# Six PSUM banks shared out anew in a cross-attention loop: four for scores, two for maxima, and one exponential instruction per key chunk

## The chip, the cores and the metric

The kernel runs on one core of a Trainium2 chip. The time is the duration of the whole program on the device in microseconds. Before the change its median is 2073.19 us of 3 runs (2069.59 to 2075.86).

## What is computed

Four transformer-like layers work on x (16 batches x 56 tokens x 128 features), a condition vector per batch, and a context of 16 batches x 1500 keys x 128. Layer 0 has a one-head attention over the context and a small mixture of experts. Layers 1, 2 and 3 each hold a cross-attention of 16 heads of 8 features over the 1500 keys; layers 2 and 3 have a self-attention and a feed-forward part as well. The cross-attentions are what the change touches. In layer 3:

```python
def mha(q_in, k_in, v_in, qw, qb, kw, kb, vw, vb, ow, ob):
    Q = (q_in @ qw + qb).reshape(Bq, Lq, H, DH)          # 16 x 56 x 16 x 8
    K = (k_in @ kw + kb).reshape(Bq, Lk, H, DH)          # 16 x 1500 x 16 x 8
    V = (v_in @ vw + vb).reshape(Bq, Lk, H, DH)
    scores = jnp.einsum('bqhd,bkhd->bhqk', Q, K) / np.sqrt(DH).astype(np.float32)
    attn = jax.nn.softmax(scores, axis=-1)
    out = jnp.einsum('bhqk,bkhd->bqhd', attn, V).reshape(Bq, Lq, D)
    return out @ ow + ob

x = _L1_xcond_ref(x, ctx_1024, cond_1024, ...)   # cross-attention
x = _L2_xcond_ref(x, cond_1024, ctx_1024, ...)   # self, cross, feed-forward
x = _L3_xcond_ref(x, ctx_1024, cond_1024, ...)   # self, cross, feed-forward
```

## The kernel before

Every engine has its own instruction list, written out in one fixed order, and semaphores join the lists. There is no scheduler: an engine that waits at an instruction holds back everything behind it.

A cross stage (`cross`, once per layer 1, 2, 3) treats 16 batches one after another. While batch b is attended, the maxima of batch b+1 ("following") are found, and the keys and values of batch b+2 ("behind") are prepared. The loop `attend` has C = 12 slots, one per chunk c of 125 keys. Its parts:

- **Scores** (`scores`, L1119). Per chunk, 4 matmuls of 224 columns, one for each group of 4 heads, write 125 keys x 896 (head, token) columns. The 896 columns are two halves of HR = 448, and each half fills most of one PSUM bank. The halves go round a ring of SC_RING = 3 banks (banks 0 to 2): half u of chunk c is in bank (2c + u) % 3. A half waits (L1117) until the exponential that read its bank last is done.
- **Exponentials** (`ACT.Exp`, L768). ScalarE takes each half out of PSUM into `probs` (an SBUF ring of 4 chunks, named `q_parts` in the trace) with one instruction: two per chunk. No maximum is subtracted here; it is already within the scores, through two more rows of the stacked queries `q_st`.
- **Values** (`values`, L1093). 8 small matmuls per chunk (16 instructions) add the chunk's part of the output into bank 6. At every even slot from 2 on, the values of the two chunks before it are done together.
- **Maxima** (`unit`, L1069 on TensorE, L1528 on VectorE). For batch b+1, 24 matmuls of 112 x 500 scores, each into a bank of a ring of MX_RING = 3 (banks 3 to 5); VectorE reduces each bank to a column of maxima with one `tensor_reduce` (L1528). Unit u waits (L1068) until the reduction of unit u - 3 is done. How many units a slot has is set by `MAXES = [2, 3, 2, 3, 2, 2, 3, 2, 3, 2, 0, 0]`; below I number a batch's units 0 to 23. The first unit of a slot stands right behind the slot's scores, the others at the slot's end, before the next slot's scores.
- **Shift** (`shift`, L1078, L1546). In slot 11 the maxima become the two extra rows of `q_st`.
- **Preparation** (`misc`, L982, L987, L993). Nine steps through bank 7: T0, T1, T2 turn the context round (TensorE L982, taken out by ScalarE L696 or L699), K0, K1, K2 make the keys (L987, taken out by ScalarE L704 as k_hi and VectorE L1435 as k_lo), V0, V1, V2 the values (L993, ScalarE L708). Each step waits until the one before it has been taken out. `SLOT_MISC` gives the slots: T0 to T2 in slots 1 to 3, K0 and K1 in 4 and 5, K2 in 7, V0 in 8, V1 in 10, and V2 in slot 0 of the next batch.
- **Joining** (`join_pair`, L1106). In slot 6 of every second batch the outputs of two batches are put together.

Before a stage's loop, `first` runs the 24 units of batch 0 in a row. The last batch of a stage has no following batch, so it has scores, exponentials and values alone. The waits that the change rewrites are L1117 (scores), L768's own wait (L767), L1086 (values) and L1068 (units).

Of the kernel before, what the change touches and what calls it, by code (L numbers as in the profile page):

```python
# [8 lines left out]
ACT = mybir.ActivationFunctionType  # L9
# [6 lines left out]
KC = S // C  # L16
# [6 lines left out]
GW = HG * T  # L23
# [3 lines left out]
HR = R // 2  # L27
# [5 lines left out]
RING = 4  # L33
UNITS = NP * NT


SC_RING = 3
MX_BANK, MX_RING = 3, 3
PV_BANK = 6
MISC_BANK = 7  # L40

# [56 lines left out]
def build(nc, x, cond, ctx, w, out, layers=4):  # L98

    with ExitStack() as stack:  # L100
        sems = {}

        def sem(name):
            if name not in sems:
                sems[name] = stack.enter_context(nc.semaphore(name))
            return sems[name]
# [4 lines left out]
        PS = stack.enter_context(nc.psum_tensor("PS", [128, 8, 512], F32))  # L111
# [9 lines left out]
        for name in VECTORS:  # L121
            place[name] = nv
            n = 1
# [73 lines left out]
        probs = q_parts[0:KC, 0:RING * R].rearrange("p (n r) -> p n r", n=RING)  # L197
# [19 lines left out]
        def ge(eng, name, value=1):  # L217

            if not (isinstance(value, int) and value <= 0):
                eng.wait_ge(sem(name), value)  # L220
# [62 lines left out]
        def by_batch(t):  # L283
            return t[:, :].rearrange("p (b t) -> p b t", b=B)
# [9 lines left out]
        def cross_of(layer):  # L294
            if layer == 1:
                return dict(n=0, norm=0, mod=True, kw=W["L1_xcond_Wkv"][:, 0, 0:D], vw=W["L1_xcond_Wkv"][:, 0, D:2 * D],
                            kb=col("L1_xcond_bkv", 0), vb=col("L1_xcond_bkv", 1),
                            ow=W["L1_xcond_Wp"][:, 0, :], ob=col("L1_xcond_bp"))
            if layer == 2:
                return dict(n=1, norm=1, mod=False, kw=W["L2_xcond_W_kvc"][:, 0, 0:D],  # L300
                            vw=W["L2_xcond_W_kvc"][:, 0, D:2 * D],
                            kb=col("L2_xcond_b_kvc", 0), vb=col("L2_xcond_b_kvc", 1),
                            ow=W["L2_xcond_W_cproj"][:, 0, :], ob=col("L2_xcond_b_cproj"))
            return dict(n=2, norm=None, mod=False, kw=W["L3_xcond_ca_kw"][:, 0, :], vw=W["L3_xcond_ca_vw"][:, 0, :],
                        kb=col("L3_xcond_ca_kb"), vb=col("L3_xcond_ca_vb"),
                        ow=W["L3_xcond_ca_ow"][:, 0, :], ob=col("L3_xcond_ca_ob"))
# [300 lines left out]
        def _(act):  # L607
# [73 lines left out]
            def preparation(layer):  # L681

                cr = cross_of(layer)
                n0 = B * cr["n"]

                def misc(batch, k, bank=MISC_BANK):
                    b, i, p = batch
                    n = n0 + b
                    kind, t = MISC[k]
                    if kind == "T":  # L690
                        act.wait_ge(sem("cxT_ready"), NT * n + t + 1)
                        dst = cxT[:, TK * t:TK * t + TK]
                        if cr["mod"]:
                            if t == 0:
                                act.wait_ge(sem("mod_copied"), b + 1)
                            act.activation(dst, PS[:, bank, 0:TK], ACT.Identity, scale=mod_b[:, p, 0:1],  # L696
                                           bias=mod_b[:, p, 1:2]).then_inc(sem("cxT_done"), 1)
                        else:
                            act.activation(dst, PS[:, bank, 0:TK], ACT.Copy).then_inc(sem("cxT_done"), 1)  # L699
                    elif kind == "K":  # L700
                        act.wait_ge(sem("k_ready"), NT * n + t + 1)

                        ge(act, f"k_stacked{PIECE_OF[t]}", STACKED * n)
                        act.activation(k_hi[:, TK * t:TK * t + TK], PS[:, bank, 0:TK], ACT.Identity, bias=cr["kb"])\  # L704
                           .then_inc(sem("k_hi_done"), 1)
                    else:
                        act.wait_ge(sem("v_ready"), NT * n + t + 1)
                        act.activation(v_sb[:, p, TC * t:TC * t + TC, :, 0:2 * DH],  # L708
                                       PS[0:KC, bank, :].rearrange("p (c r d) -> p c r d", c=TC, r=NP), ACT.Copy)\
                           .then_inc(sem("v_done"), 1)  # L710

                return misc
# [30 lines left out]
            def cross(layer):  # L743
                cr = cross_of(layer)
                n0 = B * cr["n"]
                misc = preparation(layer)

                act.wait_ge(sem("cq_done"), layer)
                ge(act, "q_first", 16 * 3 * NG * (layer - 1))
                ge(act, "q_stacked", 16 * 3 * NG * (layer - 1))  # L750
                ge(act, "dve_consts", DVE_CONSTS)
                for lo, hi in Q_PARTS:
                    for h in range(HG):
                        act.activation(qh_all[:, lo:hi, h, :], by_batch(A[7])[:, lo:hi, :], ACT.Copy, scale=mask[:, h:h + 1])\
                           .then_inc(sem("q_high"), 1)
                act.wait_ge(sem("q_first"), 16 * 3 * NG * layer)
                act.wait_ge(sem("q_stacked"), 16 * 3 * NG * layer)

                def attend(batch, following, behind, _):
                    b, i, p = batch  # L760
                    for c in range(C):
                        n = C * (n0 + b) + c
                        if c == 0 and following:
                            misc(following, SLOT_MISC[0][1])
                        ge(act, "pv_done", n - (RING - 1))
                        for u in range(2):
                            act.wait_ge(sem("scores_ready"), 2 * n + u + 1)  # L767
                            act.activation(probs[:, c % RING, u * HR:(u + 1) * HR],  # L768
                                           PS[0:KC, (2 * c + u) % SC_RING, 0:HR], ACT.Exp).then_inc(sem("exp_done"), 1)
                        if c and c in SLOT_MISC and behind:  # L770
                            misc(behind, SLOT_MISC[c][1])

                pipeline(act, lambda: None, attend)

            def self_attention(layer):
# [50 lines left out]
        def _(pe):  # L826
            mm = pe.matmul
# [14 lines left out]
            for k in range(RT):  # L842
                last = pe.transpose(PS[:, k // 4, (k % 4) * PW:(k % 4) * PW + PW], xrows[:, k, :], ident[0:PW, 0:PW])
# [35 lines left out]
            for name, m in MODS:  # L879
                for j in range(m):  # L880
                    rhs = condT if name.startswith("L3") else siluT
                    last = mm(PS[:, 6, k * B:(k + 1) * B], W[name][:, 0, j * D:(j + 1) * D], rhs[:, :],
                              start=True, stop=True)
# [158 lines left out]
            def cross(layer):  # L1042
# [39 lines left out]
                def values(batch, c):  # L1082

                    b, i, p = batch
                    n = C * (n0 + b) + c
                    pe.wait_ge(sem("exp_done"), 2 * (n + 1))  # L1086
                    if c % TC == 0:
                        pe.wait_ge(sem("v_done"), NT * (n0 + b) + c // TC + 1)
                    if c == 0:
                        ge(pe, "attn_read", n0 + b)  # L1090
                    for r in range(NP):
                        j, k = r % 4, r // 4
                        last = mm(PS[32 * j:32 * j + VW, PV_BANK, k * PW:k * PW + PW], v_sb[:, p, c, r, :],  # L1093
                                  probs[:, c % RING, r * PW:r * PW + PW], start=(c == 0 and k == 0), stop=(c == C - 1),
                                  skip_group_check=True)
                    last.then_inc(sem("pv_done"), 1)
# [13 lines left out]
                def scores(batch, c):  # L1110
                    b, i, p = batch
                    n = C * (n0 + b) + c
                    if c == 0:
                        pe.wait_ge(sem(f"q_loaded{p}"), 16 * (B // 2 * cr["n"] + i + 1))
                        pe.wait_ge(sem("shift_done"), n0 + b + 1)
                    for u in range(2):
                        ge(pe, "exp_done", 2 * n + u + 1 - SC_RING)  # L1117
                        for g in range(2 * u, 2 * u + 2):
                            last = mm(PS[0:KC, (2 * c + u) % SC_RING, (g % 2) * GW:(g % 2) * GW + GW],  # L1119
                                      k_st[0:ROWS, p, g, c * KC:(c + 1) * KC], q_st[0:ROWS, p, g, :], start=True, stop=True)  # L1120
                        last.then_inc(sem("scores_ready"), 1)

# [138 lines left out]
            for k in range(RT):  # L1261
                last = pe.transpose(PS[0:PW, 4 + k // 4, (k % 4) * D:(k % 4) * D + D], X[:, k * PW:(k + 1) * PW], ident[:, :])
# [455 lines left out]
```

## Time and profile before

| What | Value |
|---|---|
| Median of 3 runs | 2073.19 us |
| Profiled execution, its own time | 2065.48 us |
| Span of its trace | 2063.6 us |
| TensorE matmul busy | 1729.7 us, 84% |
| VectorE busy | 1261.6 us, 61% |
| ScalarE busy | 994.5 us, 48% |
| GpSimd busy | 406.5 us, 20% |

Busy times are those of the one profiled execution. In "xN" rows of the timeline N instructions of one kind are merged; their "us" runs from the first start to the last end. TensorE's matmuls overlap: a unit (L1069) shows about 0.38 us but the next matmul starts 0.21 us behind it, and the next after a scores matmul 0.10 us behind. Reductions overlap too: each shows 0.67 or 0.68 us, and in a row they start 0.59 us apart. The trace is not in slots; a slot is found from the order of its rows. The first batches of a stage start some 20 us behind the stage's first unit; the three stages run from about 380 to 810 us, 977 to 1412 us and 1590 to 2024 us.

### The profile page before, as it was taken

Reading aid. Unit: us, or ns where it says so; the run is one execution under the profiler, and the core shown is the slowest. Engines: PE = TensorE matmul, PEld = TensorE weight load, DVE = VectorE, ACT = ScalarE, POOL = GpSimd, SP = SyncE. Lnnn points to the kernel's source line nnn. Section 1 sums busy time; section 2 is a strip of 40 time slices with the busy share of each in tenths; the row PEclk is TensorE's granted clock in tenths of the full one; section 3 lists DMA queues with packets and bytes.
Section 4 is the critical chain, followed back from the end, with each engine's and each line's share of the span. In section 5 each row is a group of like instructions: output and inputs, shape, how many; then the busy total and the mean of one; then the engine's idle time right before and its main releaser. Section 6 shows DMA issues by size and latency. Waiting matters only on the chain.

```text
span 2063.6 us, 49011 instructions
## 1 busy us (share of the span) xinstructions
PE 1729.7 (84%) x18191; PEld 1152.2 (56%) x18191; DVE 1261.6 (61%) x2445; ACT 994.5 (48%) x1875; POOL 406.5 (20%) x609
## 2 busy tenths in 40 slices
PE   6888877699999988784899999997785889999986
PEld 4565534366666665442566666664342666666663
DVE  3455343577777774454777777772555777777762
ACT  1344232266666664332465666663231556666652
POOL 4000422033333313243033333300230000000000
PEclk9799978599999998796799999998885899999998
DMA  5121011332222221021322223220022233322210
GB/s 174 46 75 70 20 37 38 70 90 83 84 84 82 81 65 50 9 67 31 78 84 86 85 82 84 80 79 1 6 71 53 65 88 88 88 83 84 69 41 10
DMA packets 116117, 137.24 MB, mean 67 GB/s; under 512 B 60063, under 2 KB 106466, under 8 KB 116002
## 3 DMA queue, kind: packets, MB, share of 16 engines
q1 hardware_dynamic: 114418, 134.58, 22.9%
q8 instruction: 79, 1.29, 0.3%
q10 hardware_dynamic: 1008, 1.05, 0.2%
q14 instruction: 36, 0.29, 0.0%
q0 software_dynamic: 576, 0.02, 0.0%
HBM read 55.03 MB, written 0.46 MB: 27 GB/s over the span
## 4 chain that ended last, share of the span: by engine, by line
PE 63%; DVE 12%; issue 8%; SPq 7%; ACT 6%; DMA 3%; POOL 1%; DVEq 0%; ACTq 0%; POOLq 0%
PE PS L1069 10%; PE PS L1093 8%; PE PS L1119 8%; PE PS L987 6%; PE PS L993 6%; PE PS L833 6%; SPq L408 6%; DVE mx L1528 3%; PE PS L912 3%; PE PS L1202 2%; PE PS L982 2%; PE PS L930 2%; DMA k_st<-k_lo 2%; ACT k_hi L704 2%; PE PS L903 1%
## 5 line engine op out<-in xcount | busy, mean ns | idle before, releaser
L1528 DVE TENSOR_REDUCE mx<-PS 112x1 f32<-112x500 f32 x1152 | 715.3, 671 | 203.9 <-PE PS L1069 201.2
L768 ACT ACTIVATE q_parts<-PS 125x448 f32<-125x448 f32 x1152 | 555.8, 544 | 271.2 <-PE PS L1119 269.7
L1069 PE MATMUL PS<-k_st,q_mx 96*112 96x500 f16 x1152 | 436.8, 409 | 86.0 <-DMA q_mx<-q_all 44.5
L564 POOL TENSOR_SCALAR cx<-cx,norm_b 125x128 f32<-125x128 f32 x384 | 303.1, 812 | 586.7 <-DMA cx<-in_ctx 456.9
L1119 PE MATMUL PS<-q_st,k_st 98*125 98x224 f16 x2304 | 326.3, 264 | 22.6 <-ACT q_parts L768 21.1
L1119 PEld LDWEIGHTS PS<-q_st,k_st 98*125 98x125 f16 x2304 | 260.8, 137 | 118.0 <-ACT q_parts L768 60.1
L1093 PE MATMUL PS<-q_parts,v_sb 125*18 125x112 f32 x9216 | 293.9, 261 | 2.3 <-ACT q_parts L768 1.3
L1069 PEld LDWEIGHTS PS<-k_st,q_mx 96*112 96x112 f16 x1152 | 144.3, 132 | 211.0 <-issue 122.3
L1093 PEld LDWEIGHTS PS<-q_parts,v_sb 125*18 125x18 f32 x9216 | 209.1, 98 | 76.2 <-ACT q_parts L768 47.8
L708 ACT ACTIVATE v_sb<-PS 125x512 f32<-125x512 f32 x144 | 87.0, 604 | 257.2 <-PE PS L993 253.7
L1435 DVE SCALAR_TENSOR_TENSOR k_lo<-PS,vec,k_hi 128x500 f16<-128x500 f32 x144 | 106.2, 737 | 97.2 <-ACT k_hi L704 97.2
L704 ACT ACTIVATE k_hi<-PS,vec 128x500 f16<-128x500 f32 x144 | 97.5, 677 | 63.5 <-PE PS L987 63.5
L982 PE MATMUL PS<-ident,cx 125*128 125x125 f32 x576 | 89.3, 278 | 9.1 <-ACT cxT L696 7.5
L1546 DVE CAST q_st<-PS 2x896 f16<-2x896 f32 x48 | 52.7, 1097 | 59.8 <-PE PS L1078 59.8
L982 PEld LDWEIGHTS PS<-ident,cx 125*128 125x128 f32 x576 | 70.9, 144 | 28.0 <-ACT cxT L696 11.9
L784 ACT ACTIVATE A<-A 56x896 f32<-56x896 f32 x32 | 30.4, 949 | 93.1 <-DVE A L1629 93.1
L1367 DVE TENSOR_REDUCE neg<-PS 56x1 f32<-56x1500 f32 x16 | 27.4, 1711 | 77.1 <-PE PS L912 77.1
L1202 PE MATMUL PS<-q_parts,A 128*56 128x448 f32 x128 | 72.4, 655 | 0.0
L653 ACT ACTIVATE k_st<-PS,neg 56x1500 f32<-56x1500 f32 x16 | 24.1, 1506 | 89.1 <-DVE neg L1370 89.1
L1626 DVE TENSOR_REDUCE s_mx<-PS 56x16 f32<-56x896 f32 x32 | 34.6, 1083 | 52.2 <-PE PS L1202 52.1
L993 PE MATMUL PS<-L_xcond_Wkv,cxT 128*125 128x128 f32 x384 | 54.2, 286 | 14.3 <-issue 10.9
L912 PE MATMUL PS<-cxT,qk_b 128*56 128x500 f32 x96 | 55.3, 723 | 11.2 <-ACT cxT L639 11.2
(262 smaller groups left out, 1940.6 us busy)
## 6 DMA issues: line engine op xcount, KB each, us to landing
cx<-in_ctx SPq DMA_DIRECT2D x56, 750.0 KB
k_st<-k_hi SPq DMA_DIRECT2D x384, 62.5 KB, 2.4
k_st<-k_hi SPq DMA_DIRECT2D x384, 31.2 KB, 1.9
k_st<-k_lo SPq DMA_DIRECT2D x192, 62.5 KB, 2.0
q_mx<-q_all SPq DMA_DIRECT2D x48, 168.0 KB, 2.7
q_st<-q_all SPq DMA_DIRECT2D x48, 168.0 KB, 2.7
q_all<-q_parts SPq DMA_DIRECT2D x36, 196.0 KB, 4.1
v_sb<-in_ctx SPq DMA_DIRECT2D x8, 750.0 KB
```

What stands on the lines that cost most here:

```text
L408: sp.dma_start(k_st[32 * c:32 * c + 32, p, g, lo:hi], src[32 * g:32 * g + 32, lo:hi])\
L564: last = pool.tensor_scalar(cx[:, p, c, :], cx[:, p, c, :], norm_b[:, p, 0, c:c + 1], norm_b[:, p, 1, c:c + 1], ALU.subtract, ALU.mult)
L704: act.activation(k_hi[:, TK * t:TK * t + TK], PS[:, bank, 0:TK], ACT.Identity, bias=cr["kb"])\
L768: act.activation(probs[:, c % RING, u * HR:(u + 1) * HR], PS[0:KC, (2 * c + u) % SC_RING, 0:HR], ACT.Exp).then_inc(sem("exp_done"), 1)
L833: last = mm(dst[:, u, :], wt, r(u), start=(k == 0), stop=(k == len(rows) - 1))
L982: last = pe.transpose(PS[:, bank, c * KC:(c + 1) * KC], cx[:, p, TC * t + c, :], ident[0:KC, 0:KC])
L987: mm(PS[:, bank, 0:TK], cr["kw"], cxT[:, TK * t:TK * t + TK], start=True, stop=True)\
L993: last = mm(PS[0:KC, bank, c * D:(c + 1) * D], cxT[:, k0:k0 + KC], cr["vw"], start=True, stop=True)
L1069: mm(PS[0:PW, MX_BANK + u % MX_RING, 0:TK], q_mx[0:96, p, rb // 2, (rb % 2) * PW:(rb % 2) * PW + PW], k_st[0:96, p, rb // 2, TK * t:TK * t ...
L1093: last = mm(PS[32 * j:32 * j + VW, PV_BANK, k * PW:k * PW + PW], v_sb[:, p, c, r, :], probs[:, c % RING, r * PW:r * PW + PW], start=(c == ...
L1119: last = mm(PS[0:KC, (2 * c + u) % SC_RING, (g % 2) * GW:(g % 2) * GW + GW], k_st[0:ROWS, p, g, c * KC:(c + 1) * KC], q_st[0:ROWS, p, g, : ...
L1528: dve.tensor_reduce(mx[:, rb, t:t + 1], PS[0:PW, MX_BANK + u % MX_RING, 0:TK], AX.X, ALU.max)\
```

## The change

The six banks 0 to 5 are split 4 + 2 instead of 3 + 3. Banks 0 to 3 hold two whole chunks of scores (chunk c in banks 2(c % 2) and 2(c % 2) + 1), banks 4 and 5 the units of the maxima. One exponential of 896 columns over two neighbouring banks replaces two of 448. The scores of chunk c wait once, for the exponential of chunk c - 2; unit u waits for the reduction of unit u - 2.

```diff
-SC_RING = 3
-MX_BANK, MX_RING = 3, 3
+SC_RING = 2
+MX_BANK, MX_RING = 4, 2
 PV_BANK = 6
@@ ScalarE, attend
                         ge(act, "pv_done", n - (RING - 1))
-                        for u in range(2):
-                            act.wait_ge(sem("scores_ready"), 2 * n + u + 1)
-                            act.activation(probs[:, c % RING, u * HR:(u + 1) * HR],
-                                           PS[0:KC, (2 * c + u) % SC_RING, 0:HR], ACT.Exp).then_inc(sem("exp_done"), 1)
+                        act.wait_ge(sem("scores_ready"), 2 * n + 2)
+                        act.activation(probs[:, c % RING, :].rearrange("p (u r) -> p u r", u=2),
+                                       PS[0:KC, 2 * (c % SC_RING):2 * (c % SC_RING) + 2, 0:HR], ACT.Exp)\
+                           .then_inc(sem("exp_done"), 1)
@@ TensorE, values
-                    pe.wait_ge(sem("exp_done"), 2 * (n + 1))
+                    pe.wait_ge(sem("exp_done"), n + 1)
@@ TensorE, scores
+                    ge(pe, "exp_done", n + 1 - SC_RING)
                     for u in range(2):
-                        ge(pe, "exp_done", 2 * n + u + 1 - SC_RING)
                         for g in range(2 * u, 2 * u + 2):
-                            last = mm(PS[0:KC, (2 * c + u) % SC_RING, (g % 2) * GW:(g % 2) * GW + GW],
+                            last = mm(PS[0:KC, 2 * (c % SC_RING) + u, (g % 2) * GW:(g % 2) * GW + GW],
                                       k_st[0:ROWS, p, g, c * KC:(c + 1) * KC], q_st[0:ROWS, p, g, :], start=True, stop=True)
                         last.then_inc(sem("scores_ready"), 1)
```

On TensorE the order of the work stays and the register work for the waits changes. These are the slots 0 and 1 of a batch inside the loop: a unit, the scores of chunks 0 and 1, the first unit of slot 1 (L220 sets up a wait against a counter; L980 belongs to T0). Before:

```order
L1069 MATMUL PS<-k_st,q_mx 112x500
L220 ISA
L1119 MATMUL PS<-q_st,k_st 125x224 x2
L220 REGISTER_ALU
L1119 MATMUL PS<-q_st,k_st 125x224 x2
L220 ISA
L1119 MATMUL PS<-q_st,k_st 125x224 x2
L220 REGISTER_ALU
L1119 MATMUL PS<-q_st,k_st 125x224 x2
L1069 MATMUL PS<-k_st,q_mx 112x500
L220 REGISTER_ALU
L980 REGISTER_ALU
```

And after the change:

```order
L1069 MATMUL PS<-k_st,q_mx 112x500
L220 ISA
L1119 MATMUL PS<-q_st,k_st 125x224 x8
L220 REGISTER_ALU
L1069 MATMUL PS<-k_st,q_mx 112x500
L220 REGISTER_ALU
L980 REGISTER_ALU
```

The eight scores matmuls of the two chunks stand in the same place, with no wait set up between the halves.

On ScalarE, the first slots of layer 1's stage, where L696 takes T0, T1, T2 out and L704 K0. Before:

```order
L768 ACTIVATE q_parts<-PS 125x448 x4
L696 ACTIVATE cxT<-PS,mod_b 128x500
L768 ACTIVATE q_parts<-PS 125x448 x2
L696 ACTIVATE cxT<-PS,mod_b 128x500
L768 ACTIVATE q_parts<-PS 125x448 x2
L696 ACTIVATE cxT<-PS,mod_b 128x500
```

And after the change:

```order
L767 ACTIVATE q_parts<-PS 125x896 x2
L696 ACTIVATE cxT<-PS,mod_b 128x500
L767 ACTIVATE q_parts<-PS 125x896
L696 ACTIVATE cxT<-PS,mod_b 128x500
L767 ACTIVATE q_parts<-PS 125x896
L696 ACTIVATE cxT<-PS,mod_b 128x500
```

Two exponentials become one in each slot; the places of the preparation steps between them are the same.

## Rows read from the trace of the kernel before

**Rows 1.** Layer 2's stage: length, PE, PEld, DVE, ACT, POOL busy; clock, DMA, GB/s.

```profile
1000.00:1370.00 370.00, 340.23 (x4387) 247.37 (x4385) 271.92 (x469) 229.38 (x457) 115.06 (x166) 1.00 0.28 79
```

**Rows 2.** Group of the page: busy, mean ns | idle before, releaser.

```profile
L768 ACT ACTIVATE q_parts<-PS 125x448 f32<-125x448 f32 x1152 | 555.8, 544 | 271.2 <-PE PS L1119 269.7
```

**Rows 3.** Timeline of VectorE: start, us, instruction; the casts that end three shifts.

```profile
1237.72 1.10 DVE L1546 CAST q_st<-PS 2x896 f16<-2x896 f32 x1 [1.31 <-PE PS L1078]
...
1263.49 1.10 DVE L1546 CAST q_st<-PS 2x896 f16<-2x896 f32 x1 [1.31 <-PE PS L1078]
...
1290.93 1.10 DVE L1546 CAST q_st<-PS 2x896 f16<-2x896 f32 x1 [1.30 <-PE PS L1078]
```

**Rows 4.** Timeline of TensorE matmuls, slots 0 to 2 of that batch.

```profile
1240.49 0.74 PE L1119 MATMUL PS<-q_st,k_st 98*125 98x224 f16 x6
1241.56 0.41 PE L1119 MATMUL PS<-q_st,k_st 98*125 98x224 f16 x2 [0.33 <-ACT q_parts L768]
...
1242.45 0.59 PE L1069 MATMUL PS<-k_st,q_mx 96*112 96x500 f16 x2
...
1243.25 0.38 PE L1069 MATMUL PS<-k_st,q_mx 96*112 96x500 f16 x1
1243.47 0.59 PE L982 MATMUL PS<-ident,cx 125*128 125x125 f32 x4
```

**Rows 5.** Timeline of VectorE there: reductions of units 2 and 3.

```profile
1242.22 0.68 DVE L1528 TENSOR_REDUCE mx<-PS 112x1 f32<-112x500 f32 x1 [0.85 <-PE PS L1069]
...
1242.86 0.68 DVE L1528 TENSOR_REDUCE mx<-PS 112x1 f32<-112x500 f32 x1
```

**Rows 6.** Timeline of ScalarE there: four exponentials, then T0 taken out.

```profile
1240.97 1.84 ACT L768 ACTIVATE q_parts<-PS 125x448 f32<-125x448 f32 x4
1242.67 0.63 ACT L699 ACTIVATE cxT<-PS 128x500 f32<-128x500 f32 x1
```

**Rows 7.** Timeline of TensorE, slots 6 to 9 of that batch.

```profile
1252.80 0.91 PE L1069 MATMUL PS<-k_st,q_mx 96*112 96x500 f16 x2
...
1253.93 0.38 PE L1069 MATMUL PS<-k_st,q_mx 96*112 96x500 f16 x1
...
1256.74 1.11 PE L993 MATMUL PS<-L_xcond_W_kvc,cxT 128*125 128x128 f32 x8 [0.78 <-issue]
...
1259.52 0.76 PE L1069 MATMUL PS<-k_st,q_mx 96*112 96x500 f16 x2
```

**Rows 8.** Timeline of VectorE there: reductions of units 13, 14, 20, 21.

```profile
1252.57 0.67 DVE L1528 TENSOR_REDUCE mx<-PS 112x1 f32<-112x500 f32 x1
1253.15 0.67 DVE L1528 TENSOR_REDUCE mx<-PS 112x1 f32<-112x500 f32 x1
...
1259.12 0.68 DVE L1528 TENSOR_REDUCE mx<-PS 112x1 f32<-112x500 f32 x1 [1.32 <-PE PS L1069]
1259.72 0.67 DVE L1528 TENSOR_REDUCE mx<-PS 112x1 f32<-112x500 f32 x1
```

**Rows 9.** Groups with 896 columns: ScalarE from SBUF, VectorE from two PSUM banks.

```profile
L784 ACT ACTIVATE A<-A 56x896 f32<-56x896 f32 x32 | 30.4, 949 | 93.1 <-DVE A L1629 93.1
...
L1629 DVE TENSOR_TENSOR A<-PS,s_mx 56x896 f32<-56x896 f32 x32 | 34.7, 1083 | 3.2
```

**Rows 10.** Timeline of TensorE, last batch of layer 2's stage.

```profile
1396.57 0.96 PE L1093 MATMUL PS<-q_parts,v_sb 125*18 125x112 f32 x32
1397.46 0.79 PE L1119 MATMUL PS<-q_st,k_st 98*125 98x224 f16 x6
...
1398.90 0.96 PE L1093 MATMUL PS<-q_parts,v_sb 125*18 125x112 f32 x32
```

**Rows 11.** First 24 units of layer 1's stage: timeline of both engines, and a window.

```profile
379.89 13.77 PE L1069 MATMUL PS<-k_st,q_mx 96*112 96x500 f16 x24 [14.68 <-DMA q_mx<-q_all]
...
380.56 3.60 DVE L1528 TENSOR_REDUCE mx<-PS 112x1 f32<-112x500 f32 x6 [8.16 <-PE PS L1069]
...
383.00:394.00 11.00, 10.64 (x19) 3.01 (x18) 11.00 (x19) 0.00 (x0) 0.00 (x0) 0.50 0.80 171
```

## The prediction

> **What bounds the kernel now.** First the window over a steady stretch of a cross stage, since these three stages hold three fifths of the span and the change touches nothing else. TensorE is busy 340 of 370 us (92%) at the full granted clock, VectorE 73%, ScalarE 62% [rows 1]: TensorE's list sets the pace. The group of the exponentials says the same from the other side: ScalarE sits idle 270 us ahead of its exponentials, for the scores from TensorE [rows 2]. So a stall on TensorE counts in full, and time saved on ScalarE counts only where TensorE waits for ScalarE. Then the casts give the period: 25.77 us for a batch without a joining, 27.44 us for the next with one [rows 3]. Last I follow one batch, from 1237.72 us on, and look at each place where TensorE waits for a bank, now or under the new rings.
>
> **What the wider score ring removes.** In slot 0 the scores of chunks 0 and 1 stand in a row. Six matmuls run, the seventh and eighth, the second half of chunk 1, wait for the first exponential. One matmul lasts 0.26 and six last 0.74, so they start (0.74 - 0.26)/5 = 0.097 apart; the seventh could start at 1240.49 + 6 x 0.097 = 1241.07 and starts at 1241.56, 0.49 us late [rows 4]. It is the only such wait of a batch in the steady part; in all other slots two or three other steps lie between two scores. With two whole chunks of banks it is gone.
>
> **What one exponential costs.** Four halves in a row take from 1240.97 to the next instruction at 1242.67: 0.425 us each, 0.85 per chunk, though one alone shows 0.544 [rows 2, 6]. The overlap of neighbours is 0.12. No row shows 896 columns out of two banks on ScalarE. Lower end: ScalarE's 896 columns from SBUF, 0.949 us; upper end: VectorE's 896 columns from two PSUM banks, 1.083 us [rows 9]. I take 0.95, the same engine: less the overlap 0.83 per chunk, 0.02 less than now. That saving is on no path, since ScalarE is idle 38%. The start is later, because one instruction must wait for both halves: about 0.2 us where ScalarE is idle, 0.09 in slot 0, where the fourth scores matmul ends at 1240.49 + 3 x 0.097 + 0.26 = 1241.04, released by 1241.06, and the first half starts at 1240.97 now [rows 4, 6].
>
> The Trainium skill ("ScalarE: Activation LUTs", section "What ACT_TABLE_LOAD costs") gives an ACTIVATE with immediate scale and bias 186 ns plus 0.833 ns per element, and an overlap of about 93 ns between neighbours. As an estimate from that page, two of 448 cost 932 ns and one of 896 costs 839 ns in a row, a saving of 93 ns per chunk. The trace has 850 ns for the two, not 932, since its overlap is larger. By the page the sum below would be the same, the saving being on no path; as a rival it is number 2.
>
> **What the narrower maxima ring adds.** A unit that waited for a bank starts 0.05 us behind the reduction's end (unit 16 at 1252.80 + 0.91 - 0.42 = 1253.29, the reduction of unit 13 ends at 1253.24) [rows 7, 8]. Now take two banks, and ask at each unit whether the reduction two before it has ended.
> - Place A, units 4 and 5 (around the scores of chunk 2). Unit 4 starts at 1242.66 (the second of the pair at 1242.45); the reduction of unit 2 ends at 1242.90, so it must wait until 1242.95: 0.29. Unit 5, now at 1243.25 + 0.29 = 1243.54, needs unit 3's reduction, 1243.54 + 0.05: 0.05 more. Together 0.34 [rows 4, 5].
> - Place B, units 9 and 10 around chunk 4, repeats A: 0.34. In batches with a joining unit 17 waits in the same way, 0.34.
> - Place C, units 15, 16, 17 in batches without a joining. Unit 15 at 1252.80 needs unit 13's reduction, 1253.24 + 0.05: 0.49. Unit 16, 1253.29 + 0.49 = 1253.78, needs unit 14's, 1253.82 + 0.05: 0.09. Unit 17, 1253.93 + 0.58 = 1254.51, waits no more. Together 0.58 [rows 7, 8].
> - Place D, units 22 and 23. Unit 22 at 1259.52 needs unit 20's, 1259.80 + 0.05 = 1259.85: 0.33. Unit 23, at 1259.52 + 0.76 - 0.42 = 1259.86 plus 0.33, needs unit 21's, 1260.39 + 0.05 = 1260.44: 0.25. Together 0.58 [rows 7, 8].
>
> VectorE gives nothing back: its reductions there run back to back, and the delayed units still arrive before it is free. Behind a waiting unit on TensorE stand the next slot's scores, then a preparation step; ScalarE and VectorE get them later, and both have idle time, so the price is TensorE's own.
>
> Can a later wait of TensorE swallow this? The large one, 0.78 us of idle before V0 at 1256.74, waits for K2 to be taken out, and K2 is itself issued behind unit 17 [rows 7]: it moves along. In slots 0 to 2 the chain over ScalarE does matter: the gain of 0.49 and the loss of 0.34 at place A would put T1 at 1243.47 - 0.15 = 1243.32, but T1 needs T0 taken out, which ends at 1242.67 + 0.63 = 1243.30, or 1243.35 by the 0.09 later start less 2 x 0.02, plus 0.05 for the release: 1243.40 [rows 4, 6]. I count gain and place A together as zero (ends: 0.15 gained if T0 comes out earlier, 0.25 lost if the new exponential takes 1.083 twice). The exponential of chunk 11 ends 0.2 later than now and the last values wait for it, but TensorE idles there anyway until the cast.
>
> Sum of a batch: without a joining 0 + 0.34 + 0.58 + 0.58 = 1.50; with one 0 + 0.34 + 0.34 + 0.58 = 1.26. A stage has 15 batches with units, 8 without and 7 with a joining: 12.0 + 8.8 = 20.8 us. Three stages: 62 us.
>
> **The ends of a stage.** The first 24 units run at a granted clock of 0.50, the lower level, and the first reduction starts 0.67 us behind its matmul; reductions follow each 0.585 us (24 matmuls in 13.77) [rows 11]. With two banks a bank's round is 0.05 + 0.67 + 0.68 = 1.40 us for two units, 0.70 each: 22 x 0.115 = 2.5 us more, 7.6 in three stages. The last batch has no units and TensorE waits for exponentials in each pair of chunks: the period is 2.33 us, from 1396.57 to 1398.90 [rows 10]. TensorE's own work there is 8 x 0.097 + 0.89 (values, to the start of the next scores) = 1.67, ScalarE's 2 x 0.83 = 1.66; each still waits a little for the other. I take 2.0, halfway: 5 pairs x 0.33 x 3 = 5 us gained (ends 0 and 10).
>
> Sum: 62 + 7.6 - 5 = +65 us. The profiled execution took 2065.5, so 2130.5; the median of the runs lies 7.7 us above it, so the time to expect beside 2073.2 is 2138 us, +3.1%.
>
> **The rivals.** Times are on the footing of the median.
> 1. The other sign: the score ring's wait is what counts and the reductions keep up. It would free 0.49 in each of 45 batches, 22 us, and 5 in the last ones: 2046 us. For it: TensorE waits there in every batch. Against: at places B, C and D the reduction of two before ends after the unit's start, and no idle time of TensorE lies between them and the batch's end that starts from something earlier. It turns round if the four places cost under 0.6 us a batch together. 6%.
> 2. ScalarE sets the pace and fewer instructions count: 576 chunks x 0.02 us = 12 us on top of rival 1, 2034 us. Against: 62% busy. 2%. By the figures of the Trainium skill's page "ScalarE: Activation LUTs" the saving would be an estimated 576 x 0.093 = 54 us instead of 12, and the time 1992 us.
> 3. The waits fall half into slack (a batch loses 0.3 to 0.8, by reductions that start sooner after a delay, or by a wait of TensorE that starts from something earlier than the stall): 45 x 0.55 + 3 = 28 us, about 2101 us, 9%. A full balance, within 6 us of 2073: 4%. I call within 0.3% (6 us) no change; that is about what this kernel's runs can tell.
> 4. The waits grow: the two-bank exponential takes 1.083 or more, and T1, T2 and K0, which wait for what stands behind it on ScalarE, come 0.4 us later in each batch: 45 x 0.4 = 18 on top, 2156, and more if it costs more. For it: T1 stands within 0.1 us of this chain in my own sum. Against: in slots 3 to 5 values or a longer stretch of work lie between. 8%, half of it under 2160.
> 5. The granted clock swings. TensorE's idles grow by 1.3 to 1.5 us a batch; were half of each batch at 0.50 (as the first 24 units, 0.115 us a unit dearer), 45 x 24 x 0.115 / 2 = 62 us come for the units alone, 2200 in all. Against: 1.00 over 370 us with idles of 0.78 us in each batch [rows 1, 7, 11]. 1%. The Trainium skill ("TensorE: Matmul & The Clock Gate", section "A second HAM failure mode: psum-queue depth-cycling") says that cycling through PSUM banks with short idles between groups of matmuls can make the clock swing between its levels; by that rule, the trace before should already show it, and it does not.
>
> **How the numbers follow.** My forecast holds 70%. Its own range: the ends of place A (-0.15 to +0.25 a batch, -7 to +11 us), of the last batches (-5 to +5), and one of places B to D off by 0.3 a batch (14 us): 2115 to 2160. With the greater part of rival 3 and half of rival 4 the range goes from 2090 to 2160, 80%. Faster: rivals 1 and 2, 8%. Same: 4%. Slower: 88%.
>
> **What would show it.** Idle of TensorE's L1069 put down to the reductions (L1528) should grow from units 9, 10, 15 to 17, 22, 23; the wait of L1119 for exponentials should be nearly gone; the exponential should show 0.95 us; the casts should lie 27.3 and 28.7 us apart; the first 24 units should take 16.3 us instead of 13.8. It is wrong if the casts stay at 25.8 and 27.4 apart, or if the clock in the steady part is under 1.00.

## The result: slower by 3.4%, and the profile after

| | Before | After |
|---|---|---|
| Median, runs on the same chip | 2071.39 us (4 runs) | 2140.72 us (4 runs, 2138.88 to 2146.81) |
| Ratio, 95% interval | | 1.0342 (1.0307 to 1.0378) |
| Profiled execution, its own time | 2065.48 us | 2146.81 us |

The profiled execution is the longest of the four, so its trace has 6 us more than the median. The page of the changed kernel, the groups that answer to [rows 2, 9] (busy, mean ns of one, idle before):

```profile
L1528 DVE TENSOR_REDUCE mx<-PS 112x1 f32<-112x500 f32 x1152 | 723.7, 674 | 214.0 <-PE PS L1069 212.2
L767 ACT ACTIVATE q_parts<-PS 125x896 f32<-125x896 f32 x576 | 521.7, 917 | 375.3 <-PE PS L1119 374.6
L1069 PE MATMUL PS<-k_st,q_mx 96*112 96x500 f16 x1152 | 460.9, 418 | 135.3 <-DVE mx L1528 47.8
```

The exponential takes 0.917 us, less than both ends that I had set, and ScalarE sits idle 375 us ahead of it instead of 271. A page counts matmuls; the waits for a bank stand mostly ahead of the weight load that comes before each matmul. So I ask for the line of the units, first before and then after: who kept its engine idle, us in total, times.

```profile
  DVE mx L1528: 71.0, 233
```

```profile
  DVE mx L1528: 221.9, 633
```

TensorE's idle time ahead of a unit, put down to a reduction, rose from 71 us to 222 us. Now the batch that answers to [rows 3, 4, 7, 8]. Its casts on VectorE (start, us):

```profile
1280.17 1.10 DVE L1546 CAST q_st<-PS 2x896 f16<-2x896 f32 x1 [1.87 <-PE PS L1078]
...
1307.49 1.10 DVE L1546 CAST q_st<-PS 2x896 f16<-2x896 f32 x1 [1.87 <-PE PS L1078]
```

27.32 us for this batch against 25.77 for the one at the same place before [rows 3]. TensorE's timeline in it, slots 0 to 4:

```profile
1282.95 0.93 PE L1119 MATMUL PS<-q_st,k_st 98*125 98x224 f16 x8
1283.72 0.38 PE L1069 MATMUL PS<-k_st,q_mx 96*112 96x500 f16 x1
...
1284.36 0.92 PE L1069 MATMUL PS<-k_st,q_mx 96*112 96x500 f16 x2
...
1285.51 0.42 PE L1069 MATMUL PS<-k_st,q_mx 96*112 96x500 f16 x1
1285.79 0.65 PE L982 MATMUL PS<-ident,cx 125*128 125x125 f32 x4
...
1288.70 0.76 PE L1069 MATMUL PS<-k_st,q_mx 96*112 96x500 f16 x2
...
1289.89 0.42 PE L1069 MATMUL PS<-k_st,q_mx 96*112 96x500 f16 x1
1290.14 1.01 PE L987 MATMUL PS<-cxT,L_xcond_W_kvc 128*128 128x500 f32 x2
```

The eight scores matmuls run through: the wait at 1241.56 of [rows 4] is gone. The pair at 1284.36 takes 0.92 instead of 0.59, a wait inside it (place A). And slots 6 to 9:

```profile
1296.12 0.42 PE L1069 MATMUL PS<-k_st,q_mx 96*112 96x500 f16 x1 [0.42 <-DVE mx L1528]
1296.71 0.42 PE L1069 MATMUL PS<-k_st,q_mx 96*112 96x500 f16 x1 [0.17 <-DVE mx L1528]
...
1297.35 0.38 PE L1069 MATMUL PS<-k_st,q_mx 96*112 96x500 f16 x1
...
1303.28 0.42 PE L1069 MATMUL PS<-k_st,q_mx 96*112 96x500 f16 x1 [0.17 <-DVE mx L1528]
1303.86 0.42 PE L1069 MATMUL PS<-k_st,q_mx 96*112 96x500 f16 x1 [0.17 <-DVE mx L1528]
```

Units 15 and 16 (place C) and 22 and 23 (place D) wait for a reduction, unit 17 does not. I count each instruction's start from the batch's cast in both traces, from unrounded times, so that a figure can differ by 0.01 from the rows shown; the difference between the traces then says what each place cost:

| Up to | Before | After | Later by |
|---|---|---|---|
| unit 2 (scores wait gone) | 4.08 | 3.54 | -0.54 |
| unit 5 (place A) | 5.53 | 5.33 | -0.20 |
| T1 | 5.75 | 5.62 | -0.13 |
| unit 8 | 8.54 | 8.53 | -0.01 |
| K0 (place B) | 9.60 | 9.97 | +0.37 |
| unit 17 (place C) | 16.21 | 17.17 | +0.96 |
| unit 23 (place D) | 22.14 | 23.69 | +1.55 |
| next cast | 25.77 | 27.32 | +1.55 |

At the start of layer 1's stage, the first units on TensorE, which answer to [rows 11]:

```profile
380.68 1.25 PE L1069 MATMUL PS<-k_st,q_mx 96*112 96x500 f16 x2 [0.35 <-DVE mx L1528]
382.12 1.25 PE L1069 MATMUL PS<-k_st,q_mx 96*112 96x500 f16 x2 [0.19 <-DVE mx L1528]
383.56 1.25 PE L1069 MATMUL PS<-k_st,q_mx 96*112 96x500 f16 x2 [0.19 <-DVE mx L1528]
```

Two units take 1.44 us, 0.72 each, where they took 0.585. From the first unit to the first cast it is 19.49 us instead of 16.43, in all three stages.

### The profile page after: what moved, and what is told of

The parts are those of the page before. It is cut to its first block, busy times and chain, and to the rows that moved or that the text cites. A ratio compares the mean times of both kernels' runs of the same rounds, so it can differ in the third digit from the quotient of the medians.

```text
span 2145.0 us, 47700 instructions
## 1 busy us (share of the span) xinstructions
PE 1773.7 (83%) x18191; PEld 1155.1 (54%) x18191; DVE 1270.5 (59%) x2445; ACT 966.9 (45%) x1299; POOL 408.9 (19%) x609
## 4 chain that ended last, share of the span: by engine, by line
PE 59%; DVE 15%; issue 8%; SPq 7%; ACT 6%; DMA 3%; POOL 1%; DVEq 0%; ACTq 0%; POOLq 0%
PE PS L1069 10%; PE PS L1093 8%; DVE mx L1528 7%; PE PS L987 6%; PE PS L1119 6%; SPq L408 6%; PE PS L993 6%; PE PS L833 6%; PE PS L912 3%; PE PS L1202 2%; DMA k_st<-k_lo 2%; PE PS L930 2%; ACT k_hi L704 2%; PE PS L903 1%; PE PS L982 1%
## 5 line engine op out<-in xcount | busy, mean ns | idle before, releaser
L1528 DVE TENSOR_REDUCE mx<-PS 112x1 f32<-112x500 f32 x1152 | 723.7, 674 | 214.0 <-PE PS L1069 212.2
L767 ACT ACTIVATE q_parts<-PS 125x896 f32<-125x896 f32 x576 | 521.7, 917 | 375.3 <-PE PS L1119 374.6
L1069 PE MATMUL PS<-k_st,q_mx 96*112 96x500 f16 x1152 | 460.9, 418 | 135.3 <-DVE mx L1528 47.8
L1119 PE MATMUL PS<-q_st,k_st 98*125 98x224 f16 x2304 | 312.4, 262 | 2.3 <-ACT q_parts L767 2.1
L1093 PE MATMUL PS<-q_parts,v_sb 125*18 125x112 f32 x9216 | 301.1, 264 | 10.8 <-ACT q_parts L767 6.7
L704 ACT ACTIVATE k_hi<-PS,vec 128x500 f16<-128x500 f32 x144 | 97.5, 677 | 69.2 <-PE PS L987 65.1
```

Source lines behind the costliest of these rows:

```text
L767: act.activation(probs[:, c % RING, :].rearrange("p (u r) -> p u r", u=2), PS[0:KC, 2 * (c % SC_RING):2 * (c % SC_RING) + 2, 0:HR], ACT.Exp)\
L1069: mm(PS[0:PW, MX_BANK + u % MX_RING, 0:TK], q_mx[0:96, p, rb // 2, (rb % 2) * PW:(rb % 2) * PW + PW], k_st[0:96, p, rb // 2, TK * t:TK * t ...
L1119: last = mm(PS[0:KC, 2 * (c % SC_RING) + u, (g % 2) * GW:(g % 2) * GW + GW], k_st[0:ROWS, p, g, c * KC:(c + 1) * KC], q_st[0:ROWS, p, g, : ...
L1528: dve.tensor_reduce(mx[:, rb, t:t + 1], PS[0:PW, MX_BANK + u % MX_RING, 0:TK], AX.X, ALU.max)\
```

## The experiments

All times below are medians; "before" was run again beside each group and came to 2067.55 (e1 to e4), 2070.23 (e5 to e8) and 2070.05 us (e9, e10). The changed kernel was not run again, so a few us between it and an experiment say little. A steady batch is the one without a joining that I follow above.

**e1, the maxima ring alone.** In the kernel before:

```diff
-MX_BANK, MX_RING = 3, 3
+MX_BANK, MX_RING = 4, 2
```

> Before, with the maxima ring cut from three banks to two (banks 4 and 5; bank 3 lies unused); scores in three half-chunk banks and two exponentials per chunk as before. My theory (the ring of two costs 0.34 + 0.34 + 0.58 + 0.58 us in a batch without a joining, and the score side gives back only what place A costs): a batch is 1.8 us longer without a joining and 1.6 with one, the first 24 units 3 us longer, together 45 x 1.7 + 9 = 86 us more than before, 2157 us, and a little slower than the changed kernel (by 10 to 16 us). Rival a (the freed exponential wait is worth its full 0.49 us a batch in the changed kernel): slower than the changed kernel by 22 us or more. Rival b (the single late exponential itself costs much of the 69 us): this kernel is clearly faster than the changed one, near 2110 us.

Measured: 2153.72 us, 1.0403 (1.0353 to 1.0452) of before. A steady batch takes 27.62 us, 1.85 more than before and 0.30 more than in the changed kernel. The ring of two alone makes the whole loss and more. By the medians the score side gives back about 13 us, which fits my theory's 10 to 16 better than rival a's 22, but the interval is 10 us wide on either side; the steady batch decides it, with 0.30 given back of the 0.49. Rival b is out.

**e2, four half-chunk banks, two exponentials.** In the kernel before:

```diff
-SC_RING = 3
-MX_BANK, MX_RING = 3, 3
+SC_RING = 4
+MX_BANK, MX_RING = 4, 2
```

> The changed kernel's banks (four for scores, two for maxima) with two exponentials per chunk, one per half, as before: the ring of scores has four half-chunk banks. My theory: ScalarE's saving is on no path, and the earlier start of the first half is worth less than 0.1 us a batch, so the time is the changed kernel's within 6 us (2137 to 2147 us). Rival a (fewer instructions on ScalarE pay): slower than the changed kernel by 12 us or more. Rival b (the late start of the single exponential costs): faster than it by 10 us or more.

Measured: 2139.90 us, 1.0341 (1.0294 to 1.0387); a steady batch takes 27.33 us, as in the changed kernel. Halving the number of exponentials does nothing to a steady batch, and nothing to the time that these medians can tell. In the last batch of a stage it does cost something, 0.8 us a stage, as told below.

**e3 and e4, short reductions.** The same edit in the kernel before (e3) and in the changed one (e4); each reduction reads 125 of its 500 columns, so three quarters of the maxima are left out:

```diff
-dve.tensor_reduce(mx[:, rb, t:t + 1], PS[0:PW, MX_BANK + u % MX_RING, 0:TK], AX.X, ALU.max)\
+dve.tensor_reduce(mx[:, rb, t:t + 1], PS[0:PW, MX_BANK + u % MX_RING, 0:KC], AX.X, ALU.max)\
```

> Before, with each reduction of maxima over 125 of its 500 columns (three quarters of the maxima are left out), so that VectorE takes about 0.28 us instead of 0.67 and no unit waits for a bank. My theory: the ring's waits of before (0.28 us a batch on average) go, and the first 24 units get shorter by 4 us a stage: 45 x 0.28 + 12 = about 25 us faster than before, 2046 us. It is the yardstick for the next run.

> The changed kernel with the same short reductions (125 of 500 columns, three quarters of the maxima left out). The ring of two banks then costs next to nothing, and what is left between this run and the one before it is the score side alone (four banks, one exponential). My theory: the score side's 0.49 us of slot 0 is taken away by the chain over T0 and T1 and by unit 8's wait for its keys, so this run is 0 to 8 us faster than the short reductions on the kernel before. Rival a (the 0.49 us counts in full): 22 to 27 us faster. Rival b (the late exponential costs): slower than it by 10 us or more. If instead the maxima ring is not what costs, it stays near 2115 us or above.

Measured: e3 2037.75 us, 0.9857 (0.9813 to 0.9900); e4 2048.55 us, 0.9912 (0.9886 to 0.9938). A reduction took 0.286 us in e3. With short reductions the change costs 11 us instead of 69, so some 58 us hang on the length of a reduction. But e4 is not faster than e3, as I had it, it is 11 us slower, and rival b's threshold is touched. The greater part of it is no exponential's doing: it lies in the first 24 units of a stage, where none runs. TensorE at the start of layer 1's stage, in e3 and then in e4:

```profile
379.71 8.59 PE L1069 MATMUL PS<-k_st,q_mx 96*112 96x500 f16 x24 [14.68 <-DMA q_mx<-q_all]
```

```profile
375.57 12.69 PE L1069 MATMUL PS<-k_st,q_mx 96*112 96x500 f16 x24 [14.68 <-DMA q_mx<-q_all]
```

The ring of two still costs there with short reductions, 4.1 us in this stage and 14.0 us in the three up to the first cast. I had put it at next to nothing. The loops of the two traces differ by 9.0 us (1195.4 against 1186.4), the last batches give 1.8 back; the traces lie 16 us apart, 5 more than the medians. In steady batches the difference is small: 25.40 against 25.34, and 27.37 against 27.29 with a joining. That makes some 4 of the 9 us; the rest, near the ends of the stages, I did not take apart. TensorE in e4, slots 0 to 2:

```profile
1224.67 0.93 PE L1119 MATMUL PS<-q_st,k_st 98*125 98x224 f16 x8
...
1227.52 0.65 PE L982 MATMUL PS<-ident,cx 125*128 125x125 f32 x4 [0.25 <-ACT cxT L699]
```

and ScalarE there:

```profile
1225.26 1.73 ACT L767 ACTIVATE q_parts<-PS 125x896 f32<-125x896 f32 x2
1226.87 0.59 ACT L699 ACTIVATE cxT<-PS 128x500 f32<-128x500 f32 x1
```

Up to unit 5, e4 is 0.57 us ahead of e3. T1 then waits for T0 to be taken out, which ends at 1227.46, and starts at 1227.52; 0.16 of the lead is left. At unit 8 it is 0.00. Behind that, the values of slot 6 take 0.10 longer in e4. So the exponential wait is worth nothing in this loop.

**e5, the units spread.** In the changed kernel:

```diff
-MAXES = [2, 3, 2, 3, 2, 2, 3, 2, 3, 2, 0, 0]
+MAXES = [2, 2, 3, 2, 3, 2, 2, 2, 3, 2, 1, 0]
@@ TensorE, attend, behind misc
+                        if len(tiles) == 2 and c % 2 == 0:
+                            unit(following, tiles.pop(0))
                         if c and c % 2 == 0:
@@ VectorE, attend, ahead of k_low
+                        if tiles:
+                            unit(following, tiles.pop(0))
                         if c in SLOT_MISC and not SLOT_MISC[c][0] and behind:
```

> The changed kernel with its units spread: two or three per slot as 2, 2, 3, 2, 3, 2, 2, 2, 3, 2, 1, 0; in an even slot of three the second unit stands between the preparation step and the values, and VectorE does a slot's second reduction before k_lo instead of behind it. No unit then wants a bank while the reduction two before it is still running. My theory (bunched units make the ring of two cost 1.5 us a batch): the waits at places B, C and D go (0.34 + 0.58 + 0.58 without a joining), place A's gives nothing since T1 and unit 8 wait for other things, the first 24 units stay 3 us longer: 2141 - 45 x 1.1 to 1.3 = 2082 to 2092 us. Rival (the cost lies in having two banks at all, or in the single exponential): above 2125 us.

Measured: 2089.53 us, 1.0091 (1.0069 to 1.0113), a steady batch 25.92 us. Same banks, same single exponential, another order of units: 51 us of the 70 are gone. It is bunched units on a short ring that cost, not two banks as such. The new order is not free of waits, as I had it: units 20, 21 and 22 stand with only scores between them, and unit 22 comes 0.34 us late.

```profile
1270.66 0.42 PE L1069 MATMUL PS<-k_st,q_mx 96*112 96x500 f16 x1 [0.17 <-DVE mx L1530]
```

The spread alone was not run on the kernel before; e7 to e10 compare the two splits of the banks with the same order in both.

**e6, T0 first.** In the changed kernel's list of ScalarE:

```diff
+                        if c == 1 and behind:
+                            misc(behind, SLOT_MISC[c][1])
                         ge(act, "pv_done", n - (RING - 1))
...
-                        if c and c in SLOT_MISC and behind:
+                        if c > 1 and c in SLOT_MISC and behind:
```

> The changed kernel with one swap on ScalarE: in slot 1 T0 is taken out ahead of chunk 1's exponential instead of behind it. My theory: the swap frees T1 by 0.1 to 0.4 us, but unit 8 three steps on waits for its keys, whose copies SyncE starts only when the last scores of the batch before are done, so the batch keeps its length: within 5 us of the changed kernel. Rival (only the chain over T0 takes the 0.49 us away): 45 x 0.3 = 13 us faster than it, or more.

Measured: 2136.59 us, 1.0317 (1.0282 to 1.0353); 4 us below the changed kernel, inside the 5 that I gave. T1 moves from 5.62 to 5.59 us behind the cast, T2 from 7.94 to 7.86, unit 8 from 8.53 to 8.52, and the batch stays at 27.32. The run fits my theory but tests it weakly, since place A already holds T1 back: in the changed kernel T1 waits only 0.03 us for T0.

What unit 8 waits for is SyncE. The last copy ahead of it, in the kernel before and then in the changed one:

```profile
1244.14 0.60 SPq L408 DMA_DIRECT2D k_st<-k_lo  x1
```

```profile
1286.58 0.59 SPq L408 DMA_DIRECT2D k_st<-k_lo  x1
```

Issued by 7.02 us behind the cast in the one and 7.00 in the other. SyncE begins these 12 copies when the last scores of the batch before are done and needs 0.6 us for each, whatever slots 0 to 2 do. Unit 8 starts 8.52 to 8.54 us behind the cast in the kernel before, the changed one, e3, e4 and e6, though T2 ahead of it moves between 7.86 and 8.05; where it starts later, as at 8.85 in e1, TensorE itself is late.

**e7 and e8, the waits for k_lo.** Both kernels with e5's spread, and with the values of slots 6 and 8 ahead of what waits there:

```diff
+                        if c in (PAIR_SLOT, 8):
+                            if len(tiles) == 2:
+                                unit(following, tiles.pop(0))
+                            values(batch, c - 2)
+                            values(batch, c - 1)
                         if joins and c == PAIR_SLOT:
                             join_pair(i - 1, behind)
...
-                        if c and c % 2 == 0:
+                        if c and c % 2 == 0 and c not in (PAIR_SLOT, 8):
```

> The kernel before (three and three banks, two exponentials) with the spread units of e5, and on TensorE the values of slots 6 and 8 moved ahead of the joining and of V0, which wait there 0.99 and 0.94 us for k_lo. A candidate for a faster version. By the rows of before: 42 x 0.94 + 21 x 0.99 + 45 x 0.28 = 73 us faster, 1998 us; if the values only move the wait to the next step, above 2040 us.

> The same order as e7 on the changed kernel (four and two banks, one exponential). With the bunching gone the two bank splits should be nearly equal: my theory has this one slower than e7 by the first 24 units (9 us) and up to 10 us more where reductions stand behind k_lo, 2005 to 2020 us. Rival (the wider score ring pays once units no longer wait): faster than e7 by 10 us or more.

Measured: e7 (three and three) 2020.51 us, 0.9750 (0.9731 to 0.9769): faster than both kernels. e8 (four and two) 2063.35 us, 0.9964 (0.9949 to 0.9979). e7 gives 50 us of the 73 expected. A batch without a joining is 1.26 us shorter (24.50 against 25.77), about what the rows promised; one with a joining is only 1.1 shorter, where 2.2 were expected, and over 21 such batches that is the missing 23 us. The wait ahead of the joining moved on to the next step, K2, which now waits for VectorE's division behind the joining:

```profile
1254.72 1.11 PE L987 MATMUL PS<-cxT,L_xcond_W_kvc 128*128 128x500 f32 x2 [0.58 <-DVE OALL L1574]
```

e8 is 43 us behind e7, much more than I gave it; TensorE in slots 8 and 9 of e8 shows why:

```profile
1250.78 0.38 PE L1069 MATMUL PS<-k_st,q_mx 96*112 96x500 f16 x1
1251.33 0.42 PE L1069 MATMUL PS<-k_st,q_mx 96*112 96x500 f16 x1 [0.17 <-DVE mx L1535]
...
1254.69 0.42 PE L1069 MATMUL PS<-k_st,q_mx 96*112 96x500 f16 x1 [0.17 <-DVE mx L1535]
```

By moving the values I had made new bunches myself: units 17, 18, 19 and 20, 21, 22 with only scores between them. Each holds TensorE 0.33 us.

**e9 and e10, no bunch left.** MAXES now ends in 3, 1, 2, 0; the second unit of slot 8 goes between the values and V0, the second of slot 10 ahead of the values. e9 has three and three banks, e10 four and two.

> Three and three banks, as e7, with the units of slots 8 to 10 laid out once more: 3, 1, 2 in place of 3, 2, 1, the second unit of slot 8 between the values and V0, and both units of slot 10 ahead of its values. With three banks nothing waited in those slots, so it is within 6 us of e7: 2014 to 2026 us.

> The same order on four and two banks. In e8 a unit of slot 8 and one of slot 9 still wait 0.33 us each, and 0.12 is lost at K0: its steady batch is 0.75 us longer than e7's. My theory (only bunched units cost): the two waits go, a batch is 0.1 to 0.2 us longer than in e9, the first 24 units 3 us a stage; so 45 x 0.75 = 30 us of the difference of 43 shrink to under 10, and the time is 2030 to 2040 us. Rival (two banks cost wherever the units lie): it stays above 2050 us.

Measured: e9 2033.10 us, 0.9813 (0.9782 to 0.9844); e10 2035.57 us, 0.9823 (0.9795 to 0.9851). e10 is 28 us faster than e8 and level with e9, so the rival "two banks cost wherever the units lie" is out. e9 missed its mark, 13 us slower than e7. The reason, TensorE in slots 9 and 10 of e9 and then of e10:

```profile
1234.98 0.88 PE L1119 MATMUL PS<-q_st,k_st 98*125 98x224 f16 x4
1235.70 0.38 PE L1069 MATMUL PS<-k_st,q_mx 96*112 96x500 f16 x1
```

```profile
1241.52 0.55 PE L1119 MATMUL PS<-q_st,k_st 98*125 98x224 f16 x4
1241.90 0.38 PE L1069 MATMUL PS<-k_st,q_mx 96*112 96x500 f16 x1
```

With one unit alone in slot 9, the scores of chunks 9 and 10 stand close, and with three half-chunk banks the second half of chunk 10 waits 0.33 us. With four banks it does not: here the wider score ring pays, and e10's steady batch is 24.57 us against e9's 24.78. What it wins (8 us in the 45 batches of the loops) is about what the first 24 units of the three stages lose (9 us).

## Why the prediction was right

Forecast 2138 us, measured 2140.72. By its steps:

- **What bounds the kernel**: TensorE's list. Right: e2 and the changed kernel differ in nothing but the number of ScalarE's instructions, and the time stands still; e3 to e5 move TensorE's waits and the time follows.
- **The places of the maxima ring**: right in each place. B, C and D were put at 0.34, 0.58 and 0.58; the table above gives 0.38 (0.04 of it because K0 then starts 0.25 behind unit 10 instead of 0.21), 0.59 and 0.59. The batch is 1.55 longer where 1.50 was forecast. e1 and e5 show it from both sides. With a joining I had 1.26 and the batch of [rows 3] from 1263.49 on grew by 1.47: 0.16 more came in at K2, behind unit 17, which I had not in the sum.
- **Scores wait and place A cancel**: right, -0.01 at unit 8. I had named one of the two limits only. T1's wait is there, and behind it stands unit 8's wait for SyncE's copies. e4 shows the first without place A; the second I found in the trace after.
- **The exponential**: too dear, 0.95 against 0.917, without effect.
- **First 24 units**: 2.5 us a stage were forecast, 3.06 measured. A round of two units took 1.44 us, not 1.40. e4 shows the same ring with short reductions.
- **Last batch**: mis-sized. I had 1.65 us gained a stage; from the last cast to the stage's last joining it is 17.16, 17.16 and 17.88 us instead of 17.75, 17.76 and 17.76, about 0.4 on average. Values there wait for the single exponential, and two chunks take 2.17 us, where I had taken 2.0. This stretch of the changed kernel answers to [rows 10]:

```profile
1453.12 0.58 PE L1093 MATMUL PS<-q_parts,v_sb 125*18 125x112 f32 x16
1453.88 0.58 PE L1093 MATMUL PS<-q_parts,v_sb 125*18 125x112 f32 x16 [0.17 <-ACT q_parts L767]
1454.38 0.98 PE L1119 MATMUL PS<-q_st,k_st 98*125 98x224 f16 x8
```

In e2, with the same banks and two exponentials, the values run through and two chunks take 2.04 us; the same stretch from the last cast to the last joining takes 16.34 us in all three stages, 1.4 less than before. So four banks give nearly what I had forecast there, and the single exponential takes more than half of it back.

```profile
1450.74 1.20 PE L1093 MATMUL PS<-q_parts,v_sb 125*18 125x112 f32 x32
...
1452.78 1.20 PE L1093 MATMUL PS<-q_parts,v_sb 125*18 125x112 f32 x32
```

- **What the sum left out**: the 45 batches of the loop together took 73.8 us more in the two traces (1276.7 against 1202.9 us), the forecast had 62. Were every batch longer by what the steady ones of its stage are, it would be 66; the other 8 us are in a few batches, most of them near the ends of a stage, and there the wait of unit 8 grew and the clock fell, as below.

In terms of the median, 65 us were forecast and 69.3 measured. Part of this closeness is luck. The sum was made for the trace, and the two traces lie 81.3 us apart, 16 more than the sum. Its three terms were off in the same direction: the loops by about 12 us, the last batches by 4, the first 24 units by 1.6. The medians lie closer together than the traces, because the profiled execution of before is 5.9 us below its median and that of the changed kernel 6.1 above. What puts them there is not explained. The places and the sizes of the waits in a steady batch, which make up most of the forecast, are not luck.

## What to carry to other kernels

When a ring of buffers gets shorter, compare each user's start with the end of the reader that many places before it, in the trace of before; the waits within a bunch count once, by the latest of them, and no more than what the path gives. A mean busy share (VectorE 73%) says nothing on it: the price hung on the order, and spreading the users took back 51 of 70 us with the same two banks. Ahead of counting the wait that a change removes, look two or three steps further for the next chain that holds the engine, since here two of them stood ready.

## What the hardware showed that I had not expected

One exponential over two PSUM banks took 0.917 us, less than the 0.949 of the same length from SBUF. Against 0.544 for 448 columns that is 0.83 ns per further column. This agrees with the figure of 0.833 ns per element in the Trainium skill ("ScalarE: Activation LUTs", section "What ACT_TABLE_LOAD costs"). Two in a row take 1.61 us to the next instruction, 0.80 each.

The granted clock fell inside the loops for short stretches. Rival 5 had a swing over half of each batch at 1%; that did not come, but short falls did. In layer 2's stage of the changed kernel, TensorE and then two windows (length, PE, PEld, DVE, ACT, POOL busy, clock):

```profile
1373.81 0.63 PE L1069 MATMUL PS<-k_st,q_mx 96*112 96x500 f16 x2 [1.76 <-DMA k_st<-k_lo]
...
1375.38 1.87 PE L987 MATMUL PS<-cxT,L_xcond_W_kvc 128*128 128x500 f32 x2
```

```profile
1375.10:1378.50 3.40, 3.40 (x35) 1.80 (x35) 1.60 (x3) 1.41 (x2) 0.94 (x2) 0.50 0.01 3
1100.00:1370.00 270.00, 242.85 (x3047) 170.33 (x3049) 188.34 (x325) 152.72 (x202) 89.94 (x131) 1.00 0.29 82
```

TensorE had idled 1.76 us for the keys of unit 8, then waited for a reduction, and for 3.4 us was granted 0.50, its lower level of 1.2 GHz; the two matmuls of K0 took 1.87 us instead of 1.01. The loops of this trace have seven such falls of 3.4 us each, and the one at 1061 us stands behind an idle of 1.43 us for the same keys; in the 270 us of the second window there is none. By the rows of a fall beside the same rows at the full clock, I estimate its cost at 1.6 us, some 11 us for seven. The loops of the trace before have one, at 785 us, 6.8 us long. The experiments' traces have two to five each in their loops. Most lie near a stage's ends, where unit 8 waits longest; idles of that length without a fall are there too (2.18 us at 1380 us in the trace before), so the idle by itself does not decide it, and whether the longer idles brought the falls about was not tested.
